# When GpSimd loads a unit's step number and waits for its slot, in the second edge pass of a graph network on Trainium2

## The reference

```
f0 = x0 @ Wl1_0 * inv8                     # per node: 64 scalars
f1 = einsum('num,uv->nvm', x1, Wl1_1) ...  # per node: 32 vectors of 3
w  = silu(edge_scalars @ Wfc1) @ Wfc2      # per edge: 192 weights, w0..w3
e0, e1 = f0[edge_src], f1[edge_src]        # gather: 160 values per edge
mid0 = w0 * e0 * sh0
mid1 = w3 * einsum('eum,em->eu', e1, sh1) / sqrt(3)
mid2 = w1[:, :, None] * e0[:, :, None] * sh1[:, None, :]
mid3 = w2[:, :, None] * e1 * sh0[:, :, None]
n0..n3 = mean of mid0..mid3 over the edges of each target node
```

## Time and profile before

| what | value |
|---|---|
| median of three runs | 10209.57 us |
| profiled execution, its time | 10306.75 us |
| its span | 10304.9 us |
| second edge pass, first gather to start of last unit | 6961.75 to 10130.29 us |
| busy share of the span: TensorE, VectorE, ScalarE, GpSimd | 78%, 66%, 51%, 49% |
| mean granted TensorE clock | 0.813 |

### The profile page before, as it was taken

The page is one execution under the profiler, slowest core; times in us unless marked ns, Lnnn a source line. Parts: engine busy times, 40 slices in busy tenths (PEclk is TensorE's granted clock), DMA queues, the critical chain, the costliest instruction groups (busy, mean ns, idle before and its releaser), DMA issues. The chain is left out here.

```text
span 10304.9 us, 195656 instructions
## 1 busy us (share of the span) xinstructions
PE 8085.0 (78%) x43972; PEld 6348.5 (62%) x43973; DVE 6778.5 (66%) x16742; ACT 5206.1 (51%) x16950; POOL 5020.8 (49%) x5222
## 2 busy tenths in 40 slices
PE   5788888888878878878888869988777777666667
PEld 3677776777767767767777759964444443333335
DVE  7666666666666666666666778877666555555445
ACT  5545555555545444455555541157665555554444
POOL 1545555555545555455555529715444444444441
PEclk7777777777777777777777879999888888888888
DMA  7323222222222222222222228664333333333225
GB/s 231 75 71 76 76 74 74 75 76 77 76 71 76 74 73 73 71 74 76 76 74 75 77 63 250 212 125 107 95 93 92 90 89 88 86 84 83 80 80 168
DMA packets 971866, 967.97 MB, mean 94 GB/s; under 512 B 452750, under 2 KB 788750, under 8 KB 971662
## 3 DMA queue, kind: packets, MB, share of 16 engines
q0 software_dynamic: 225792, 385.65, 15.3%
q1 hardware_dynamic: 512032, 346.40, 12.2%
q10 hardware_dynamic: 233936, 234.90, 6.8%
HBM read 677.57 MB, written 288.65 MB: 94 GB/s over the span
## 5 line engine op out<-in xcount | busy, mean ns | idle before, releaser
L745 POOL DMA_INDIRECT e_g_dst<-table_dst,e_idx x1568 | 1494.0, 953 | 1791.9 <-ACT logits L898 1421.9
L2015 POOL DMA_INDIRECT f_e<-table,f_src x1568 | 1495.0, 953 | 1658.6 <-DVE f_dot L2171 830.1
L784 PE MATMUL e_ps_t<-ident,e_m 128*128 128x128 f32 (+1 forms) x7840 | 1537.8, 343 | 748.6 <-issue 425.4
L745 POOL DMA_INDIRECT e_g_src<-table_src,e_idx x1568 | 1497.2, 955 | 1015.0 <-issue 675.6
L784 PEld LDWEIGHTS e_ps_t<-ident,e_m 128*128 128x128 f32 (+1 forms) x7840 | 1177.6, 176 | 948.9 <-issue 647.5
L2070 PE MATMUL f_ps_a<-sums 128*128 128x384 f32 x3936 | 1697.7, 583 | 5.8 <-DVE sums L2170 3.4
L2070 PEld LDWEIGHTS f_ps_a<-sums 128*128 128x128 f32 x3936 | 852.9, 228 | 676.1 <-issue 395.4
L2059 PE MATMUL f_ps_w<-f_w,f_hidden 64*128 64x192 f32 x3936 | 539.5, 400 | 834.2 <-issue 421.1
L2170 DVE TENSOR_TENSOR f_ey<-f_e,f_ps_w 128x384 f32<-128x384 f32 x492 | 272.6, 554 | 1349.3 <-POOLq L1998 1170.0
L877 ACT ACTIVATE e_m1t<-e_ps_t 128x512 f32<-128x512 f32 (+1 forms) x1176 | 684.3, 598 | 899.0 <-remote 359.9
L2059 PEld LDWEIGHTS f_ps_w<-f_w,f_hidden 64*128 64x128 f32 x3936 | 367.1, 217 | 919.0 <-issue 464.1
(11 more groups left out here) (268 smaller groups left out, 18215.4 us busy)
## 6 DMA issues: line engine op xcount, KB each, us to landing
edge_values<-e_h ACTq DMA_DIRECT2D x392, 330.0 KB
r_h<-edge_values SPq DMA_DIRECT2D x196, 660.0 KB, 4.0
sums<-sums ACTq DMA_DIRECT2D x492, 192.0 KB
e_g_src<-table_src,e_idx POOLq DMA_INDIRECT x1568
e_g_dst<-table_dst,e_idx POOLq DMA_INDIRECT x1568
f_e<-table,f_src POOLq DMA_INDIRECT x1568
f_rbf<-basis SPq DMA_DIRECT2D x492, 48.0 KB
basis<-t_part SPq DMA_DIRECT2D x42, 448.0 KB, 3.1
```

The lines of the kernel that those rows point to most:

```text
L745: pool.indirect_dma_start(out=into[:, r, t, :], out_offset=None, in_=table, in_offset=bass.IndirectOffsetOnAxis(ap=idx[:, r, c:c + 1], axi ...
L784: last = nc.tensor.transpose(ps_t[bank][0:channels, t * P:(t + 1) * P], rows(t), ident[:])
L2015: pool.indirect_dma_start(out=rows_of_units[:, (place * RING + r) * T + t, :], out_offset=None, in_=table, in_offset=bass.IndirectOffsetOn ...
```

## The change

The call of `tell` for a unit no longer stands behind that unit's gathers, but ahead of the next unit's gathers, behind the next unit's load of its step number and its wait for the slot. The last unit's `tell` stands behind everything. Ahead of a part's first unit, the wait for the copied index columns (L2006) and the count on `issued` (L2007) come ahead of that `tell` as well, and so does the jump back of the loop (L2029).

```
                         pool.wait_ge(product, until * PRODUCT)
                         pool.sem_inc(issued, 1)
+                    before = part if r else part - 1
+                    started = r > 0 or not first or place > 0
+                    if started:
+                        tell((r - 1) % RING, before)
                     for t in range(T):
                         at = (RING - 1 - r) * T + t
                         pool.indirect_dma_start(
...
                     if r == 1 and not last:
                         copy(u + RING, (place + 1) % PARTS)
-                    tell(r, part)
...
             for part in range(turns * PARTS, parts):
                 fetch(part, part % PARTS, False, part == parts - 1)
+            tell(RING - 1, parts - 1)
```

## The result

The changed kernel took 9867.18 us, median of three runs (9804.08 to 9868.99), against 10209.57. The ratio of the means is 0.9643 with a 95% interval of 0.9581 to 0.9706 (the ratio of the medians is 0.9665). Forecast was 9890 us, a ratio of 0.9687: faster, for the reason given, but the saving came out larger. 0.9643 of the median before is 9845.6 us, under the low end of 9860.

What follows compares the result with a forecast made beforehand. GpSimd's serial chain of gathers, landing and load was taken to bound the pass; shortening 360 gaps from 1196.6 to 875 us saves about 320, so 10209.6 becomes 9890 us. Range 9860 to 9955, with an unlikely far end of 9987.

Steps and rivals of the forecast that it cites:

- GpSimd's closed chain bounds the pass: Gathers, landing, load and count run in series on GpSimd, 392 times, while VectorE starves for gathered rows.
- Load, multiplication and count cost 0.8 us a unit, 288 us for 360: On GpSimd's queue, between a unit's landing and the next gathers, these instructions take 0.8 us.
- the two covers: Moved load runs during gather generation, over 5 us before landing, or at least during the 1.64 us landing; cost 0.
- The jumps' 2.8 us are hidden: GpSimd's 10 loop jumps, moved ahead of the landing, have their 2.8 us covered by the remaining 3.4 us of gathers.
- The early stretch shows the gap to come, 2.41 us: The first 32 units lack load and slot wait; their 2.41 us gap was taken for later units, against 3.32.
- The sum, 320 us: GpSimd's 360 late gaps fall from 1196.6 us to 875, at 2.43 us each, saving 322, taken as 320.
- The low end, 9860: Bottom of the whole range; the forecast alone reached 9865 with gaps of 2.37 us and 15 us scatter of plain runs.
- Rival A: Cover for the moved GpSimd work is partly lost: 223 to 300 us saved, 9910 to 9987 us; chance 0.07.
- Rival B: VectorE holds up GpSimd's gathers: 388 us come back, 10278 us, or 10101 in the mild case; chance 0.03.
- Rival C: TensorE becomes the bound at its lower clock level, steps of 6.96 us: 10466 us; chance 0.02.
- Rival D: GpSimd's load waits for the landing whatever its place; gap stays 3.3 us, 10210 us; chance 0.04.
- What can be late next: VectorE and TensorE at 4.02 us a step need 1978 us against a 2850 us pass, so GpSimd stays the bound.

Runs made afterwards that it cites:

- e1: Changed kernel with the step-number load, slot wait and count on `issued` back behind `tell`; only the jump and index-copy wait stay ahead: ratio 0.9955 to the kernel before.
- e2: Changed kernel with only the slot wait, its multiplication and count on `issued` back behind `tell`, the load staying ahead: ratio 0.9733 to the kernel before.
- e5: Changed kernel measured again, unaltered, in five rounds on another occasion: 10002.97 us beside 10355.52 for the kernel before, ratio 0.9662.
- e3: Changed kernel with three more loads of the same step number ahead of `tell`: ratio 0.9631 to the kernel before.
- e6: Changed kernel with `tell` moved behind the next unit's four gathers, so two units' gathers are in flight: ratio 1.0144 to the kernel before.
- e9: e6 with SyncE's loads left out after the first four steps: ratio 1.0118 to the kernel before.

## Why the prediction was right and where it was off

- **GpSimd's closed chain bounds the pass.** Right. A late unit's period fell by 0.95 us, 0.92 of it the gap; over 359 units that is 341 of the pass's 343 us, and VectorE still starves at `landed`.
- **Load, multiplication and count cost 0.8 us a unit, 288 us for 360.** Right in kind, a little low: e1, e2 and e5 give 239.6 + 61.0 = 301 us, 0.84 a unit (317 with the first profile of the changed kernel in e5's place).
- **They are hidden.** Right, and by the stronger of the two covers that were offered. e3 rules out that only the landing covers them.
- **The jumps' 2.8 us are hidden.** Right: 25.5 us for all in e1, 28 forecast.
- **The slot wait is never the one waited for.** Right: behind `tell` (e2) it costs 0.17 us a unit, its instructions, and ahead of it nothing.
- **The early stretch shows the gap to come, 2.41 us.** Right: 2.39 us where the landing releases, 2.40 over all.
- **The sum, 320 us.** The size of this term is the first step that failed: it was too low against the first profile (343), near the second (326). What was mis-sized in it is the late gap, put at 2.43 us. It held an allowance of 0.05 us for late scatter that did not come, and measured 2.40 by the same reading: 0.03 x 359 = 11 us. The gathers themselves became 9 us shorter in all, which the sum held at nothing without a reason.
- **The low end, 9860.** This is the second step that failed: the ratio puts the time 44 us under the forecast, of which 23 are the pass, as above, and 21 are scatter; neither alone would have left the range. "Plain runs scatter by 15 us" was read from three runs. Stages that the change never touches moved the start of the pass by 95 us between the two profiles, one plain run took 9804 us, and the ratios' intervals are 1.3% and 0.6% wide. A low end that allowed for this would have been near 9800. For the same reason the 97 us by which the profiled execution before was over the median were no cost of recording, as far as this shows: after the change the profiled one took 9868.99 us beside a median of 9867.18. The far end of 9987 rested on that.
- **Rival A** did not happen (no jump over 3.11 us). **Rival B**: gathers starting at another place of VectorE's steps took 946 ns in the median, at most 1067, before 947 and 1094. The rule of the Trainium skill weighed there (SBUF — State Buffer, the box on VectorE blocking DMA) does not show in any run here. **Rival C**: the granted clock rose from 0.85 to 0.90, as closer steps had suggested. **Rival D**: the gap fell.
- **"What can be late next"** was answered rightly for this change and would have misled for the next one: 492 steps of 4.02 us on VectorE looked like 870 us of room below the changed kernel. e6 to e9 show that it can't be had by closing GpSimd's gaps: steps take 4.0 us only where gathers pause or have ended.

No version tried here is clearly faster than the changed kernel; e3's 0.9631 lies within its scatter.

## What to carry to other kernels

A stretch of the trace that lacks the step in question, here the first units into an empty ring, is a finished experiment: it gave the gap to 0.02 us. A queue that runs ahead of its engine hides register loads and even a loop's jump, if they stand ahead of the wait that stops it. Before a range is given, look at how far the untouched stages move from run to run, for that can be larger than any doubt about the change itself; and don't count an engine's idle gap as free room before a run has closed it.

## What had not been expected of the hardware

Gathers generated without a pause slow down engines that share neither data nor a queue with them. TensorE's counts are the ones that come late: ScalarE got the weights up to 21.4 us after it could have gone on (e9), 1.8 us on average, instead of at most 0.11 once the gathers had ended, while ScalarE's and VectorE's own counts stayed 0.01 us behind their instructions and the instructions of VectorE kept their length. SyncE's register instructions took 0.70 us (e6) instead of 0.03 to 0.04. With a pause of 2.4 us in each 7.2 the effect is small (mean 0.28 us), with none it costs more than the whole change had gained. One landing of four gathers takes 1.64 us from the end of their generation, and a branch back of the loop on GpSimd 2.8 to 3.0 us.
